# Nine shapes of identity matmuls on TensorE ahead of the weight transposes

## Reference

```
x = x + attention_in_windows(_gn(x), bn_gamma, bn_beta, bn_mean, bn_var, qk_w, v_w)
x = x + local_attention(_gn(x), w_out, b_out)
```

## Time and profile before

| what | us |
|---|---|
| median of the 2 timed runs | 1738.77 |
| lowest, highest of them | 1737.81, 1739.73 |
| the profiled execution, first to last instruction (span) | 1743.6 |
| TensorE busy in it | 1434.3 |
| VectorE busy | 1396.1 |
| GpSimd busy | 1139.6 |
| ScalarE busy | 1030.6 |

### The profile page before, as it was taken

The page is one execution under the profiler, slowest core; times in us unless marked ns, Lnnn a source line. Parts: engine busy times, 40 slices in busy tenths (PEclk is TensorE's granted clock), DMA queues, the critical chain, the costliest instruction groups (busy, mean ns, idle before and its releaser), DMA issues.

```text
span 1743.6 us, 62829 instructions
## 1 busy us (share of the span) xinstructions
PE 1434.3 (82%) x26281; PEld 755.6 (43%) x26281; DVE 1396.1 (80%) x1964; ACT 1030.6 (59%) x1861; POOL 1139.6 (65%) x873
## 2 busy tenths in 40 slices
PE   4989999999999999974597888879797786966754
PEld 2656666666666666651132332323233232322332
DVE  4774777777777777778999999999989999995933
ACT  3554777777777777754564747667474766543300
POOL 5333555555555555530679999999999999985700
PEclk9775999999999999987699999999999999997978
DMA  8702011111104220215202324223232522126079
GB/s 330 301 11 52 18 34 39 28 46 24 50 17 100 21 55 18 55 33 141 52 20 59 98 52 122 52 73 91 58 79 51 122 52 71 39 67 244 22 309 388
DMA packets 106870, 152.35 MB, mean 87 GB/s; under 512 B 71362, under 2 KB 83650, under 8 KB 100034
## 3 DMA queue, kind: packets, MB, share of 16 engines
q1 hardware_dynamic: 106690, 149.67, 29.4%
HBM read 77.99 MB, written 65.20 MB: 82 GB/s over the span
## 4 chain that ended last, share of the span: by engine, by line
PE 44%; DVE 18%; POOL 16%; issue 13%; ACT 5%; SPq 1%; DMA 1%; DVEq 0%; POOLq 0%; ACTq 0%
POOL arena L799 11%; PE PS L1484 7%; PE PS L1321 7%; PE PS L1330 5%; PE PS L1346 5%; DVE arena L1111 4%; PE PS L1298 4%; POOL arena L810 4%; PE PS L1290 4%; DVE arena L1107 4%; PE PS L1507 3%; PE PS L1428 3%; PE PS L1309 2%; PE PS L1360 2%; ACT arena L988 2%
## 5 line engine op out<-in xcount | busy, mean ns | idle before, releaser
L1220 DVE TENSOR_TENSOR arena<-arena,PS 128x1568 f32<-128x1568 f32 x334 | 583.9, 1777 | 16.1 <-PE PS L1484 8.3
L799 POOL TENSOR_TENSOR arena<-arena 128x1568 f32<-128x1568 f32 x168 | 517.7, 3123 | 87.7 <-PE PS L1428 68.1
L765 POOL TENSOR_TENSOR arena<-arena,consts 128x196 f32<-128x196 f32 x512 | 294.3, 609 | 283.7 <-ACT arena L849 283.7
L1484 PE MATMUL PS<-arena,consts 32*32 32x392 f32 x12800 | 396.9, 512 | 78.3 <-DVE arena L1220 23.4
L997 ACT ACTIVATE PS<-arena 128x392 f32<-128x392 f32 x334 | 166.3, 501 | 255.8 <-DVE arena L1220 255.1
L1428 PE MATMUL PS<-arena,consts 128*32 128x392 f32 x1664 | 200.3, 554 | 83.2 <-POOL arena L799 42.1
L1107 DVE TENSOR_REDUCE arena<-PS 128x8 f32<-128x392 f32 x256 | 143.2, 559 | 144.7 <-PE PS L1321 143.2
L1484 PEld LDWEIGHTS PS<-arena,consts 32*32 32x32 f32 x12800 | 145.8, 104 | 246.0 <-issue 96.1
L874 ACT ACTIVATE arena<-PS 128x512 f32<-128x512 f32 x256 | 152.9, 597 | 161.0 <-PE PS L1330 157.2
L810 POOL TENSOR_TENSOR arena<-arena 128x1568 f32<-128x1568 f32 x66 | 202.7, 3081 | 29.4 <-ACT arena L937 20.7
L1330 PE MATMUL PS<-consts,arena 128*128 128x128 f32 x1024 | 177.9, 299 | 0.2
(11 more groups left out here) (109 smaller groups left out, 1724.2 us busy)
## 6 DMA issues: line engine op xcount, KB each, us to landing
arena<-x_wide_dram SPq DMA_DIRECT2D x32, 660.0 KB, 8.2
arena<-x_wide_dram SPq DMA_DIRECT2D x256, 67.5 KB, 2.0
x_wide_dram<-arena SPq DMA_DIRECT2D x12, 1125.0 KB
arena<-in_x_dram SPq DMA_DIRECT2D x8, 1568.0 KB, 14.5
x_wide_dram<-arena SPq DMA_DIRECT2D x64, 196.0 KB, 4.3
x_dram<-arena SPq DMA_DIRECT2D x8, 1568.0 KB, 7.5
attn_dram<-arena SPq DMA_DIRECT2D x256, 49.0 KB, 3.0
arena<-x_dram SPq DMA_DIRECT2D x8, 1568.0 KB, 19.0
```

What stands on the lines that cost most here:

```text
L765: i = nc.gpsimd.tensor_tensor(k_bd[k][:, r], keys.unsqueeze(1).to_broadcast([P, HEADS_T, S]), head_mask.unsqueeze(2).to_broadcast([P, HEAD ...
L799: nc.gpsimd.tensor_tensor(tile, x_part, by, ALU.mult).then_inc(pool_tile, 1)
L1220: nc.vector.tensor_tensor(by_channel(v_tiles[n % V_RING]), shifted_values(half, k), over_channels(PS[:, 2 + n % W_BANKS, 0:PIX]), ALU.mult ...
L1484: mm = nc.tensor.matmul(PS[dst, 4 + i, 0:PIX], ident[src, src], tile[src, c * PIX:(c + 1) * PIX], start=done == 0, stop=done == NK - 1)
```

## The change

TensorE gets matmuls between its wait for the masks and its wait for the parameters. Each multiplies a block of the identity as weights with the first `width` columns of `consts` (the identity, and beyond 128 columns the start of `pair_mean`) and writes to a PSUM bank from 4 to 7 (one for each row tile) that is not read before it is written again. A set covers the array once with tiles of rows x columns; sets are repeated. Ten calls follow each other, in nine shapes, 64x64 twice: 296 matmuls, each with its weight load. Nothing else is changed.

```diff
         @block.tensor
         def _(pe):
             pe.wait_ge(masks_ready, 3)
+
+            def warm_up(rows, columns, width, sets):
+
+                moving = consts[:, 0:width]
+                for _ in range(sets):
+                    for r in range(P // rows):
+                        for c in range(P // columns):
+                            src, dst = slice(r * rows, (r + 1) * rows), slice(c * columns, (c + 1) * columns)
+                            nc.tensor.matmul(PS[dst, 4 + r, 0:width], ident[src, dst], moving[src], start=True, stop=True)
+
+            warm_up(64, 64, 196, 12)
+            for rows, columns, width, sets in ((32, 128, 144, 6), (32, 64, 144, 4), (64, 64, 144, 6), (64, 32, 144, 4),
+                                               (128, 32, 144, 5), (32, 32, 96, 3), (32, 32, 144, 3), (64, 128, 144, 5),
+                                               (128, 64, 144, 5)):
+                warm_up(rows, columns, width, sets)
             pe.wait_ge(par_loaded, 16 * 16)
```

## The result

| kernel | median us | lowest to highest | executions | ratio to before, 95% interval |
|---|---|---|---|---|
| before | 1738.77 | 1737.81 to 1739.73 | 2 | |
| changed | 1754.94 | 1753.59 to 1756.29 | 2 | 1.0096 [1.0067, 1.0126] |
| changed, second job | 1754.78 | 1744.24 to 1771.75 | 12 | 1.0076 [1.0032, 1.0119] |
| changed, third job | 1753.59 | 1741.25 to 1767.42 | 12 | 1.0078 [1.0043, 1.0113] |
| before, beside all experiments | 1739.62, 1742.05, 1740.01 | 1718.75 to 1757.14 | 87 in three jobs | |

The change makes the kernel slower by 13 to 16 us, 0.8 to 1.0%. That is within the 2% that were called no change, and clear of zero. The forecast was 1746 us. Two things stand in this table that the two runs of before hid: its single executions lie up to 21 us away from their median, and it takes a dozen of each to place a difference of 10 us.

The account below looks back on a forecast made before the run. TensorE was taken to bound the attention units. A 15.8 us warm-up ends 8.0 us behind 13.10 us; faster transposes return half a microsecond: net +7 us, 1738.8 + 7 = 1746 us, range 1724 to 1762 us (8 in 10).

Parts of the forecast that it names:

- The transposes had no slack: Weight transposes at 13.10 us: whatever moves them moves the first attention unit, through 8.36 us of small steps.
- plain shift: Everything behind the transposes moves 7 us later, low stretches about the same: 1746 us, own range 1740 to 1752, chance 0.44.
- a further low stretch: Second rival, units 0 to 7: another 41 us at low clock costs 15.5 us, giving 1761 us; chance 0.20.
- a warm-up that never rises: Warm-up at the low level throughout, 24 us of work: +16 or 1755 us, within the second rival's 0.20.
- The length of the warm-up: Added matmuls before the transposes: 15.8 us, ending at 21.1 us, with the clock rising after the first twelve sets.
- the additions for small tiles and wide weights: Warm-up beyond its column cost: +1.8 us for 32x32 tiles, +0.6 for 32x64 and 64x32, +1 for 128-column weights.
- Its upper end: Longest warm-up, 30 us of work ahead of the transposes, would shift the kernel by +22 us.
- The warmth is lost: Between transposes and first projection, 8.36 us of small steps lets the clock fall, so the warm-up brings no gain.
- The third rival: High clock survives the small-step chain and the first units run fast: 3.6 us come back, 1742 us; chance 0.05.
- Low stretches: Three stretches at 1.2 GHz before 173.2 us, costing 12.6, 15.5 and about 1.2 us: 29 us in all.
- The price per microsecond: Attention units: each us of low stretch costs 0.31 us in the first units and 0.38 in later ones.
- The drain that I weighed as a cost: Warm-up: each of nine changes of tile shape would add some tenths of a microsecond.

Follow-up runs that it names:

- `delay_matched`: Changed kernel with the warm-up left out; TensorE instead waits for 39 memsets by GpSimd before the transposes: 1756.9 us, ratio 1.0110.
- `narrow`: Changed kernel with all 296 matmuls cut to 16 columns, the rest as changed: 1747.9 us, ratio 1.0066 to the kernel before.
- `looped`: Changed kernel with each call's sets as a program loop, a quarter of the instructions, same matmuls: 1754.5 us, ratio 1.0073 to the kernel before.
- `loads_after`: Changed kernel with the seven other image loads held back until the transposes are done: 1743.7 us, ratio 1.0032 to the kernel before.
- `first_only`: Changed kernel with only the first call, 48 matmuls of 64x64 and 196 columns: 1739.8 us, ratio 1.0010 to the kernel before.
- `keep_busy`: Kernel before plus 128x128, 256-column matmuls: 22 before the parameter wait, 9 behind the transposes, 2 and 11 behind the channel means: 1743.9 us, ratio 1.0018.
- `keep_busy_fitted`: Kernel before plus 11, 4, 1 and 5 wide 256-column matmuls, fitted to TensorE's idle stretches at the start: 1725.9 us, ratio 0.9950.
- `hold_clock`: As `keep_busy_fitted`, plus filler matmuls in units 1 to 7 ahead of the transposed values, two more units written out: 1710.6 us, ratio 0.9850.
- `one_shape`: Changed kernel with all ten calls replaced by 56 sets of 64x64 tiles, 144 columns, 224 matmuls: 1751.6 us, ratio 1.0045 to the kernel before.
- `delay`: Changed kernel with the warm-up left out; TensorE instead waits for 42 memsets by GpSimd before the transposes: 1767.7 us, ratio 1.0138.
- `after_again`: The changed kernel once more, unaltered, with the kernel before in the same job: median 1754.8 us.

## Why the prediction was right, and where its size was off

**The bound and its place.** The transposes had no slack, and most of the shift came through to the end: `delay_matched` shows that a pure wait of 20.5 us costs 19 us [9, 29]. The forecast of a plain shift with low stretches of about the same total held in kind.

**The time was met in part by luck.** The shift was forecast as 7 us and was 19, and 1755 us lies outside the 1740 to 1752 us that the plain shift was given. It lies inside the wide range only because this was drawn out for a further low stretch or a warm-up that never rises, priced at 1761 and 1755 us. Neither came: the warm-up rose early, and the attention units got no further long stretch (77 us at the low level from unit 0 to unit 13, beside 85 us before, where the column misses the first units). By the sign that the prediction set itself, a warm-up of more than 18 us, it was wrong in a term.

**The length of the warm-up** is the term that was mis-sized: 15.8 us were given for it, the profile shows 27.3, of them 21.9 busy and 5.4 standing still. Most of the busy part is one mistake. I divided a group's time by its count and took the count for matmuls, "eight 64x64 matmuls" at L1290 in 0.50 us. The code issues four there; a float32 matmul leaves two records. A column of a full set then costs 2.55 ns at the high and 4.4 ns at the low level, not 1.27 and 2.2, and 8112 columns cost 20.7 us at the high level; busy time in the warm-up is 21.9 us, a third of it at half clock. The other parts of the sum erred the other way: doubled as a whole, 15.8 us would be 31.6. The rise came about 3 us into the warm-up, well before the end of the first twelve sets, and the additions for small tiles and wide weights were too dear. Rows before held the warning: the page counts 12800 at L1484, where the loops make 6400.

**Instruction delivery** was not in the sum at all: 5.4 us of standstill (4.8 and 5.7 in the second and third job's profiles), shown by `narrow`, `looped` and `loads_after`. "It adds 296 matmuls with as many weight loads on TensorE's queue alone: no DMA" missed that a program is itself fetched by DMA. Its upper end, 22 us of net shift, held all the same: 19.0, 20.7 and 19.5 us at the first projection in three profiles.

**The warmth is lost** on the way through the small-step chain: right, in both kernels and in `first_only`. The third rival was wrong for this change; `keep_busy` and `keep_busy_fitted` show what it would have needed, work behind the transposes too.

**Low stretches.** They were priced at 29 us in the profile of before and taken as a fixed property of a kernel that a shift might upset. The 87 executions of the unchanged kernel, 1719 to 1757 us, and the three profiles of the changed kernel say that the time changes from one execution to the next, in the low stretches and also behind unit 63. The two runs shown, 2 us apart, had hidden it. The profile of before needed 184.3 us to unit 13, where the changed kernel's three profiles had 176.5, 171.6 and 170.4 us. I had expected the profiled times to move by what the medians do; they moved by 11 us, the medians by 16. The price per microsecond held. Here is the stretch from unit 0 to unit 13 in the profile with the longest and in the one with the shortest (`loads_after`, then `keep_busy_fitted`):

```profile
42.92:228.26 185.34, 173.58 (x1804) 112.87 (x1805) 128.12 (x305) 107.22 (x212) 72.09 (x114) 0.73 0.35 128
```

```profile
25.97:185.02 159.05, 138.52 (x1804) 93.96 (x1805) 125.39 (x305) 108.00 (x212) 72.53 (x115) 0.96 0.44 149
```

Clocks of 0.73 and 0.96 mean 100 and 13 us at the low level; 26.3 us of time for 87 us is 0.30, beside the 0.31 that was read for the first units. And removing nearly all low stretches of the units, with a warm start, brought 26 us [17, 36] (`hold_clock`).

**Shape changes.** The drain that I weighed as a cost is not visible: `looped` passes all ten calls without a standstill. The 0.95 against 0.86 us that I had read as a sign of it is none, since both groups follow a change of shape. What the changes cost below the resolution of the groups is open.

**Open.** The first projection moved by 19 to 21 us, the medians by 13 to 16 us. Whether the difference is the spread, or the changed kernel has less low clock or a shorter end in a mean execution, three jobs don't settle. `loads_after` (14.5 us of shift, 5.6 us [-1, 12] of time) points the same way. `narrow` (13.5 and 11.5 us [5, 18]), `looped` and `one_shape` (7.6 and 7.8 us [0, 16]) fit a plain shift, and `delay` lies above it. Why the part behind unit 63 varies is open too.

## What to carry to other kernels

A warm-up helps where it reaches the first real matmuls without an idle stretch, and costs nothing only if it ends before what it covers: size it from the trace, use few wide matmuls rather than many small ones (22 of 256 columns filled 12.7 us without a stop in `keep_busy`), and fill the gaps behind it as well. Look for short idles of the engine that bounds a stage: here fillers ahead of one wait in units 1 to 7 were worth at least as much as those at the start, 15 us between the medians against 14. And before a difference of 1% is argued, run the unchanged kernel a dozen times: the spread of its own executions was 2% here.

## What the runs showed of the hardware

- A float32 matmul with float32 operands leaves two MATMUL and two LDWEIGHTS records; a transpose by the identity leaves one (four transposes at L1265, x4). A 128x128 matmul of 256 columns takes 0.43 us at 2.4 GHz, four cycles per column.
- TensorE can outrun the delivery of its own program: in straight code it stopped after 351 records and after 128 more, whatever the shape or width, 0.46 to 5.16 us at a time with bulk loads running; with them held back it ran through 479 records and then stopped for 1.66 us. Between the two stops lie 128 matmul and 128 weight-load records, and each restart comes 1.2 to 1.5 us after the end of a transfer of 16384 bytes on the instruction queue. The same matmuls from a loop had no stop.
- The granted clock of the same program differs between executions in where it falls: the changed kernel was low for 61 us at a stretch in one profile (100.7 to 162.1 us) and for 34 us at most in another (37.9 to 72.1 us, `after_again`). The clock column shows 1.00 before its first change even where the matmuls run at half speed.
- The same idle can be followed by a fall of the clock or not. In the changed kernel TensorE stood idle for 1.46 us ahead of L1324 at 72.17 us, and the clock fell at 73.4 us; it stood idle for 1.46 us again ahead of 88.14 us, and the clock held until 100.7 us.
